# Swapping the order of the mixing passes and the score passes at the head of each TensorE step of a fused attention block

## The reference

```python
x = x + layernorm(attn(layernorm(x)))
# in attn: proj(W, b) = einsum('nse,fe->nsf', x, W) + b, as (n, heads 16, tokens 2048, 32)
scores = jnp.einsum('nqhd,nkhd->nhqk', Q, K) * scale   # q, k: the 16 heads; h: the token
attn = jax.nn.softmax(scores, axis=-1)
out = jnp.einsum('nhql,nlhd->nqhd', attn, V).reshape(n, s, e)
return jnp.einsum('nse,fe->nsf', out, Wo) + bo
```

## Time and profile before

| | |
|---|---|
| time, three runs | 1689.78, 1691.34, 1692.69 us; median 1691.34 |
| span of the profiled execution, first to last instruction | 1686.3 us |
| own time of the profiled execution | not given apart from its span; the median of the runs lies 5.0 us above the span |
| granted TensorE clock, mean | 0.994 |
| busy share TensorE matmul, weight load | 98%, 78% |
| busy share VectorE, ScalarE, GpSimd | 78%, 51%, 76% |
| small matmuls in the profile | 8192 for the scores, 8192 for the mixing |

### The profile page before, as it was taken

The page is one execution under the profiler, slowest core; times in us unless marked ns, Lnnn a source line. Parts: engine busy times, 40 slices in busy tenths (PEclk is TensorE's granted clock), DMA queues, the critical chain, the costliest instruction groups (busy, mean ns, idle before and its releaser), DMA issues.

```text
span 1686.3 us, 55468 instructions
## 1 busy us (share of the span) xinstructions
PE 1657.2 (98%) x22550; PEld 1320.8 (78%) x22550; DVE 1309.6 (78%) x2455; ACT 855.4 (51%) x1730; POOL 1285.2 (76%) x1303
## 2 busy tenths in 40 slices
PE   8999999999999999999999999999999999999994
PEld 6777887877878778788877877887887887787873
DVE  7687877877877877778778778778787787787777
ACT  4355455555544544554555555445445555555453
POOL 5577877877877778778778778787787787787777
PEclk9999999999999999999999999999999999999997
DMA  7666666666666666666666666666666676666553
GB/s 252 173 172 184 176 169 171 182 178 174 166 188 170 175 175 183 172 179 179 172 170 179 180 175 166 184 175 171 173 186 170 173 187 171 173 168 189 155 139 88
DMA packets 388635, 293.46 MB, mean 174 GB/s; under 512 B 296854, under 2 KB 296854, under 8 KB 388380
## 3 DMA queue, kind: packets, MB, share of 16 engines
q1 hardware_dynamic: 345552, 223.02, 49.8%
q10 hardware_dynamic: 42828, 66.90, 13.2%
HBM read 155.46 MB, written 67.24 MB: 132 GB/s over the span
## 4 chain that ended last, share of the span: by engine, by line
PE 95%; DVE 2%; issue 1%; ACT 1%; POOL 1%; ACTq 1%; DMA 0%; DVEq 0%
PE ps_k L1080 8%; PE ps_y L1160 7%; PE ps_y L1161 7%; PE ps_v L1080 7%; PE ps_y L1164 7%; PE ps_v L1083 7%; PE ps_v L1081 7%; PE ps_q L1080 7%; PE ps_k L1081 7%; PE ps_q L1083 7%; PE ps_k L1083 7%; PE ps_q L1081 7%; PE ps_s L1121 6%; PE ps_o L1140 5%; ACTq L943 0%
## 5 line engine op out<-in xcount | busy, mean ns | idle before, releaser
L910 ACT ACTIVATE q_sb<-ps_q,mr 128x512 f32<-128x512 f32 x127 | 87.5, 689 | 537.6 <-issue 537.6
L403 POOL TENSOR_TENSOR z<-z,b_row 128x512 f32<-128x512 f32 x124 | 187.5, 1533 | 222.7 <-DVE z L679 222.7
L605 DVE STREAM_TRANSPOSE qT<-q_sb 128x512 f32<-128x512 f32 x128 | 137.6, 1075 | 107.4 <-ACT q_sb L910 106.9
L1080 PE MATMUL ps_k<-wk_hi,xT_hi 128*128 128x512 f32 x504 | 212.2, 421 | 0.3 <-issue 0.3
L1160 PE MATMUL ps_y<-wo_hi,oT_hi 128*128 128x512 f32 x504 | 200.3, 397 | 2.1 <-ACT oT_hi L926 1.9
L1161 PE MATMUL ps_y<-wo_lo,oT_hi 128*128 128x512 f32 x504 | 199.7, 396 | 0.0
L1080 PE MATMUL ps_q<-wq_hi,xT_hi 128*128 128x512 f32 x504 | 199.5, 396 | 0.0
L1081 PE MATMUL ps_k<-wk_lo,xT_hi 128*128 128x512 f32 x504 | 199.2, 395 | 0.4 <-issue 0.4
L1080 PE MATMUL ps_v<-wv_hi,xT_hi 128*128 128x512 f32 x504 | 199.4, 396 | 0.0
L383 POOL TENSOR_TENSOR x_t<-x_t,mr_row 128x512 f32<-128x512 f32 x126 | 195.7, 1553 | 4.4 <-ACT mr_row L1005 4.4
L1081 PE MATMUL ps_q<-wq_lo,xT_hi 128*128 128x512 f32 x504 | 198.9, 395 | 0.0
(11 more groups left out here) (189 smaller groups left out, 3721.0 us busy)
## 6 DMA issues: line engine op xcount, KB each, us to landing
x_in<-in_xa SPq DMA_DIRECT2D x64, 512.0 KB, 4.9
x_t<-in_xt SPq DMA_DIRECT2D x64, 512.0 KB, 4.8
k_bd<-kT SPq DMA_DIRECT2D x512, 64.0 KB, 2.4
v_d<-v_tok ACTq DMA_DIRECT2D x128, 256.0 KB, 2.2
v_key<-v_d SPq DMA_DIRECT2D x128, 256.0 KB, 3.9
res<-in_xr SPq DMA_DIRECT2D x64, 512.0 KB, 4.9
p_bd<-pT ACTq DMA_DIRECT2D x508, 64.0 KB, 2.3
out<-o_sb SPq DMA_DIRECT2D x62, 512.0 KB, 2.9
```

The lines of the kernel that those rows point to most:

```text
L403: nc.gpsimd.tensor_tensor(z[:, j, :], z[:, j, :], b_row[:, :], ALU.add).then_inc(z_done, 1)
L605: nc.vector.transpose(qT[t % 2][:, :, :].rearrange("p n h -> p h n"), q_sb[:, :].rearrange("p (h d) -> p h d", d=D)).then_inc(qT_done, 1)
L1080: nc.tensor.matmul(ps, x_hi[:, e, :], w_hi[:, e, :], start=e == 0, stop=False)
```

## The change

In the loop of TensorE's program two lines change places. `mixed(s - 2)` is now issued ahead of `scores(s - 1)`. The same matmuls run with the same operands, semaphores and counts. The queues of the other engines, the steps ahead of the loop (where the order was already this one for tile 0) and the steps behind it stay as they were.

```diff
@@ the tensor engine's program
             values(3)
             output(1)
             for s in range(4, NT - 2):
+                mixed(s - 2)
                 scores(s - 1)
-                mixed(s - 2)
                 keys(s)
                 queries(s)
                 values(s)
                 output(s - 2)
```

## The result

The change made the kernel slower by 0.7%. Its median was 1701.68 us over 4 runs, against 1690.99 us for the kernel before, measured beside it. The ratio is 1.0069, 95% interval 1.0057 to 1.0081. The forecast was 1692.5 us in a range of 1688.5 to 1696.5 us.

The account below looks back on a forecast made before the run. TensorE's own rate was taken as the bound. 0 for the burst, -0.6 at the start and +1.85 for late probabilities gave +1.2 us: span 1687.5, plus 5.0 outside it, 1692.5 us, range 1688.5 to 1696.5 us.

Parts of the forecast that it names:

- The burst itself, 0 us: Scores plus mixing on TensorE in each step: still 1.44 us in the new order, so 0 us.
- The loop's first step, -0.6 us: Loop's first burst: mixing fills the idling before tile 3's scores, keys start at 61.84; gain 0.6 us, once.
- The chain of the probabilities, +0.62 us for even and +0.39 us for odd tiles: Later scores delay the chain through VectorE and ScalarE by 0.62 us in even tiles, 0.39 us in odd; no build-up.
- The slack of the mixing, 1.28 and 1.05 us less: Margin from last probability landing to mixing: 2.6 us ordinarily, 1.3 us after; loses 1.05 or 1.28 us, cover holds.
- Losses by late probabilities, +1.85 us: Mixing waits for slow probability transfers in three of 122 steps, near 356, 1050 and 1114 us; 1.85 us in sum.
- "What is queued behind a waiting mixing is everything on TensorE; nobody else is held up that has no slack of its own": Claim that a waiting mixing delays only TensorE's own queue; no extra loss was added for it.
- the one on the slower side: Late probabilities as a rule, at each burst's head: many steps wait for slow landings; 1697 us, chance 0.09.
- The one on the faster side: Scores wait less: 1.0 us of waiting outside the first step goes, no mixing late; 1689.7 us, chance 0.17.
- From span to time, 5.0 us: Whole run: the median time of 1691.34 us lies 5.0 us above the profiled span of 1686.3 us; kept after the change.

Follow-up runs that it names:

- the changed kernel's second execution: The changed kernel run once more with nothing else edited, against the kernel before: ratio 1.0079.
- the kernel before with mr_row later: Kernel before, with the load into mr_row issued in the next even step, behind the burst instead of ahead of it: ratio 1.0008.
- the wait on the load: Changed kernel, mixing's two waits reordered so its first weight load carries the wait for the probabilities, not a separate sequencer instruction: ratio 1.0033 against the kernel before.
- stop for queries: Kernel before, scores' two waits reordered: the first weight load carries the keys' wait, the sequencer waits for the transposed queries: ratio 1.0051.
- the same with mr_row later: Kernel before with the sequencer waiting for the transposed queries, and the mr_row load issued behind the burst: ratio 1.0040 against the kernel before.
- the kernel with the stop for the probabilities: Kernel before, order kept, but the scores also wait for the probabilities that the mixing behind them needs: ratio 1.0054.
- the even steps swapped: Kernel before with mixing ahead of scores in even steps only: ratio 1.0028.

## Why the prediction was wrong

- **The burst itself, 0 us:** right. 1.44 us and a period of 12.84 us, as shown above.
- **The loop's first step, -0.6 us:** not borne out. The idling there was 1.0 instead of 1.9 us, but the burst started at 61.02 as before and the keys at 62.45, not at 61.8. In the changed kernel's second execution the idling was 1.8 us, and in the kernel before with mr_row later 0.4, so one execution differs from another by more than the term.
- **The chain of the probabilities, +0.62 us for even and +0.39 us for odd tiles:** half right. VectorE's top moved from 0.89 to 1.55 us behind the burst's start in even tiles, and stayed at 1.92 in odd ones. The last landing moved by 0.22 us (even) and 0.35 us (odd) in the median.
- **The slack of the mixing, 1.28 and 1.05 us less:** it went from 2.37 to 1.49 us in even tiles and from 1.92 to 0.93 us in odd ones, by 0.88 and 0.99 us. The 2.6 us that the forecast started from were one even tile's. The ordinary cover held, as forecast.
- **Losses by late probabilities, +1.85 us:** mis-sized. They measured 4.8 and 7.4 us in two executions of the changed kernel, and 3.8 us with the wait on the load. The step that failed is the count of three steps taken from one execution and moved by a constant. None of the three (s = 27, 81 and 86) was late in either of these two executions; others were. The landings had a longer tail: before 4.6 us at most, changed 5.4 us, in this place (the view of the tile, then the timeline).

```profile
L943 ACTq DMA_DIRECT2D p_bd<-pT x4: 514/615/682, 1479.9 to 1481.8; - x4
...
DMA to landing us min/median/max: 4.1/4.3/5.4
```

```profile
1487.24 0.85 PE L1140 MATMUL ps_o<-p_bd,v_key 64*32 64x64 f32 x64 [1.36 <-issue]
```

- **"What is queued behind a waiting mixing is everything on TensorE; nobody else is held up that has no slack of its own":** this is the sentence that failed most, worth 8.5 of the loop's 14.2 us. It counted the wait where the engine stands and not where the sequencer stands. A wait that ends 1.3 us before the engine needs it was called free, but it stops the sequencer, and the next block of instructions isn't transferred until the sequencer is past it. The forecast read neither the rows of semaphore instructions nor the line of the queue q8 on the page.
- **The rivals:** the one on the slower side had the right place and sign, but its mechanism, late probabilities as a rule, is about a third of the loss. The one on the faster side had nothing to win: the starts before show no waiting ahead of the loop's other bursts. The Trainium skill's page "Runtime: NRT & Kernel Launch", section "Instruction fetch mechanics", says that instructions come in blocks of 256 by the sequencer's own transfers and that the cost of a new block is mostly hidden. The first part agrees with the 178 transfers for 45,622 instructions. The second held in the kernel before (0.8 us) and not in the changed one (9.3 us).
- **From span to time, 5.0 us:** wherever the record has both for one execution, its time lies 1.8 to 2.0 us above its span. So the profiled execution of before was probably some 3 us faster than the median. That didn't touch the forecast difference, but it would account for spans that differ by 12.3 us and medians by 10.7.

What is shown: the idling in the keys depends on the sequencer's stop (wait on the load, stop for queries), it lies where blocks of the program end, and the late blocks' transfers start only after the stop has ended, in even steps later still by the load into mr_row. What is argued: that getting past the stop is what calls for the block. The trace has the transfer's start, not its call. Why the delay behind the stop varies from 1.1 to 4.7 us in the even steps of before stays open, and so does what makes single transfers of probabilities land late.

## What to carry to other kernels

A satisfied wait isn't a free wait on an engine that runs behind its sequencer: ask how far ahead of the engine each wait ends, above all in front of a stretch of many short instructions. Put the wait that ends last on the instruction that needs it, as its first wait in the program, and give the sequencer those that are long over. And where an idle stretch has no releaser, look at the instruction queue and at whether the places move when instructions are added.

## What the runs showed of the hardware

After one of the longer idle stretches in the keys TensorE's granted clock fell to its lower level for some 3 us. In the changed kernel's second execution it stood still from about 219.5 to 221.7 us, and by the windows view (the last three numbers are PEclk, the DMA share and GB/s) the next stretch ran at half, 1.2 GHz instead of 2.4:

```profile
219.00:222.90 3.90, 1.84 (x69) 1.52 (x54) 3.83 (x8) 2.11 (x5) 3.28 (x4) 1.00 0.25 81
222.90:226.20 3.30, 3.30 (x10) 2.56 (x9) 0.59 (x3) 2.00 (x4) 3.11 (x4) 0.50 0.62 117
```

Seven matmuls then started 0.43 us apart instead of 0.23, some 1.5 us more in all. The same followed an idle stretch of 2.2 us at 216 us in the kernel with the stop for the queries, one of 2.1 us at 1342 us in the same with mr_row later, and two in the kernel with the stop for the probabilities (3.5 us in the first step, 2.4 us at 1334 us). It didn't follow the stretches of 2.25 us at 217 us and 2.2 us at 1046 us in the first trace of the changed kernel, nor one of 2.7 us at 1042 us with the even steps swapped. So the length of the idle stretch doesn't decide it alone.
